# Turning the graph's count matrices by transposing DMAs, with four buffers for the basis loads, in a one-core graph network kernel

## The reference

```
L0: out = relu(concat(segment_sum(h1[src], dst) + img @ Wim + bim,  h1) @ Wap + bap),   h1 = h @ Wn + bn
L1: w[r] = einsum('rb,bio->rio', att, basis)[r]   # basis is 30 x 512 x 512, two relations, two sub-layers
    agg = segment_sum(msg of the edge's own type, row);   out = agg + x @ root + bias
L2: five times relu((h + segment_sum(h[src], dst)) @ W + b)
L3: segment_sum(edge_weight * (x @ weight)[src], dst) + bias
```

## Time and profile before

| | |
|---|---|
| time, median of 3 runs | 2070.17 us (2068.27 to 2072.72) |
| time of the profiled execution | 2070.58 us |
| its span | 2068.6 us |
| TensorE, VectorE, ScalarE busy | 92%, 39%, 30% of the span |
| mean granted TensorE clock | 0.969 |

### The profile page before, as it was taken

The page is one execution under the profiler, slowest core; times in us unless marked ns, Lnnn a source line. Parts: engine busy times, 40 slices in busy tenths (PEclk is TensorE's granted clock), DMA queues, the critical chain, the costliest instruction groups (busy, mean ns, idle before and its releaser), DMA issues.

```text
span 2068.6 us, 23800 instructions
## 1 busy us (share of the span) xinstructions
PE 1900.6 (92%) x7966; PEld 907.6 (44%) x7978; DVE 799.5 (39%) x1978; ACT 626.5 (30%) x1200; POOL 7.8 (0%) x27
## 2 busy tenths in 40 slices
PE   4878888589999989999999999999999999987998
PEld 2545554353333434444444444444444445433443
DVE  5666677424111162110111223354444544384122
ACT  1544544414666042111211000132232323275100
POOL 1000000000000000000000000000000000000000
PEclk9999999879999969999999999999999999998999
DMA  5889889670100052100000010700000000021011
GB/s 119 219 204 228 218 202 224 180 274 0 36 1 1 0 173 102 41 0 1 1 21 31 31 41 31 307 29 5 21 6 21 6 21 1 16 66 56 21 51 41
DMA packets 47379, 157.54 MB, mean 76 GB/s; under 512 B 9316, under 2 KB 11260, under 8 KB 38816
## 3 DMA queue, kind: packets, MB, share of 16 engines
q1 hardware_dynamic: 42880, 142.28, 23.9%
q10 hardware_dynamic: 4384, 13.78, 1.9%
HBM read 120.38 MB, written 35.65 MB: 75 GB/s over the span
## 4 chain that ended last, share of the span: by engine, by line
PE 78%; DMA 7%; DVE 5%; ACT 4%; issue 2%; DVEq 1%; another core or an unknown queue 1%; SPq 0%; POOL 0%; ACTq 0%; POOLq 0%
PE psum L1195 29%; PE psum L1181 28%; PE psum L1413 6%; DMA hs<-in_L_gnn_basis 6%; PE psum L1264 3%; PE psum L1098 2%; PE psum L1317 2%; PE psum L1364 2%; PE psum L1130 2%; PE psum L1129 1%; ACT adj L878 1%; DMA hs<-in_x 1%; DVE hs L582 1%; DVE hs L584 1%
## 5 line engine op out<-in xcount | busy, mean ns | idle before, releaser
L1195 PE MATMUL psum<-hs,adj 128*128 128x512 f16 x2880 | 643.0, 380 | 0.8 <-DVE hs L689 0.8
L1181 PE MATMUL psum<-wb,xt 128*128 128x512 f32 x1152 | 511.6, 602 | 15.5 <-DVE hs L817 13.4
L1195 PEld LDWEIGHTS psum<-hs,adj 128*128 128x128 f16 x2880 | 280.1, 98 | 354.0 <-issue 37.1
L1181 PEld LDWEIGHTS psum<-wb,xt 128*128 128x128 f32 x1152 | 219.2, 193 | 286.0 <-issue 283.9
L970 ACT ACTIVATE adj<-hs,pbias 128x512 f32<-128x512 f32 x216 | 134.5, 708 | 86.1 <-PE psum L1264 86.1
L1130 PE MATMUL psum<-hs 128*128 128x192 f32 x636 | 159.2, 333 | 0.0
L1003 ACT ACTIVATE ua<-ua 128x512 f32<-128x512 f32 x60 | 37.9, 631 | 335.3 <-DVE ua L831 187.6
L582 DVE TENSOR_SCALAR hs<-hs 128x128 f32<-128x128 f16 x318 | 89.8, 282 | 105.7 <-PE psum L1130 63.1
L1413 PE MATMUL psum<-hs,adj 128*128 128x512 f32 x288 | 123.8, 592 | 0.0
L768 DVE TENSOR_TENSOR vt<-psum,adj 128x512 f32<-128x512 f32 x24 | 16.6, 692 | 271.9 <-PE psum L1181 271.9
L1130 PEld LDWEIGHTS psum<-hs 128*128 128x128 f32 x636 | 117.0, 197 | 7.2 <-issue 1.2
(11 more groups left out here) (213 smaller groups left out, 1478.8 us busy)
## 6 DMA issues: line engine op xcount, KB each, us to landing
hs<-in_L_gnn_basis SPq DMA_DIRECT2D x64, 960.0 KB, 8.2
aw_scratch<-xt ACTq DMA_DIRECT2D x12, 768.0 KB, 5.5
adj<-aw_scratch SPq DMA_DIRECT2D x1, 9216.0 KB, 38.1
x_scratch<-adj SPq DMA_DIRECT2D x24, 256.0 KB, 2.2
hs<-x_scratch SPq DMA_DIRECT2D x24, 256.0 KB, 2.6
ts_scratch<-adj SPq DMA_DIRECT2D x1, 4608.0 KB, 17.9
as_scratch<-adj SPq DMA_DIRECT2D x1, 4608.0 KB, 30.1
adj<-ts_scratch SPq DMA_DIRECT2D x1, 4608.0 KB, 14.5
```

The lines of the kernel that those rows point to most:

```text
L1181: x = pe.matmul(psum[:, bank, :], xt[:, i, k, :], w[:, k, :], start=first and k == 0, stop=last and k == 3)
L1195: x = pe.matmul(psum[:, i % 2 + (4 * half if own else 0), :], adj[:, m, j, P * i:P * i + P], hs[:, t, half, j, :], start=n == 1 or (own an ...
```

## The change

**Turning.** A new function `turn_types` issues two transposing DMAs (`dma_start_transpose`, 128 x 1536 float16 each) from ScalarE's queue at the end of each block, from `typed` straight into `adj[:, 1]` and `adj[:, 2]`. TensorE's 24 float16 transposes and ScalarE's four copies of each block go; a block has three turn lots (weights alone) in place of six. ScalarE waits for the transposing DMAs of two blocks before (`typed_turned`) when it stages a block again.

**Buffers.** Two more chunk buffers lie in parts of `adj` that are written late; chunks 0 to 51 go through four buffers, 52 to 63 through the first two. Mixed chunks are staged in four rows in place of two.

**Ahead of the loop.** SP issues three chunk loads at once and the fourth where it issued the first two; the 16 `att` loads move to ScalarE's queue. GpSimd makes the small iotas first; VectorE starts when the edges are there and waits for constants later; `attw` is computed before the window ranges.

**Behind the loop.** The meeting at `built` goes. SP issues the first three loads of `x` when TensorE is through with all turn lots but two; the later loads and stores wait for what they overwrite or read. VectorE waits for the small vectors after the copy of line 601 in place of before it.

```diff
+        for m in (1, 2):
+            basis.append(adj[:, m, NT - 3:NT, :].rearrange("p j n -> p (j n)")[:, 0:4 * D * 2].bitcast(F32))
+        FAR_CHUNKS = 52
+
+        def basis_of(n):
+            return (n + 1) % 4 if n < FAR_CHUNKS else (n + 1) % 2
+
+        def nth_of(n):
+            return len([m for m in range(n + 1) if basis_of(m) == basis_of(n)])
+
+        def follower(n):
+            return min([m for m in range(n + 1, 64) if basis_of(m) == basis_of(n)], default=None)
...
+        spare = wb[:, :, :, :].rearrange("p a b n -> p (a b n)")[:, 2 * NT * P:2 * NT * P + 2 * D].rearrange("p (k n) -> p k n", k=2)
+        mixed = [ua[:, 0, :], ua[:, 1, :], spare[:, 0, :], spare[:, 1, :]]
...
             if s >= 0 and 1 <= q <= 3:
-                here += [("turn", s, 2 * (q - 1)), ("turn", s, 2 * (q - 1) + 1)]
+                here += [("turn", s, q - 1)]
             if u == NW - 1:
-                here += [("turn", BLOCKS - 1, n) for n in range(6)]
+                here += [("turn", BLOCKS - 1, n) for n in range(3)]
...
+            for n in range(3):
+                load_chunk(n)
             sp.wait_ge(ecol_ps, 1)
             sp.wait_ge(span_ready, 4)
-            load_chunk(0)
-            load_chunk(1)
+            load_chunk(3)
             for n in range(CH):
...
-                if n + 2 < CH:
+                if follower(n):
                     sp.wait_ge(side_ps, lot + 1)
-                    load_chunk(n + 2)
+                    load_chunk(follower(n))
                 sp.wait_ge(side_out, side_copied(lot))
...
-            sp.wait_ge(row_out, 16 * (NT + 1))
-            sp.wait_ge(built, 4)
+            sp.wait_ge(side_ps, len(side) - 2)
...
                 if g == 3:
+                    sp.wait_ge(side_ps, len(side))
+                    sp.wait_ge(typed_summed, BLOCKS)
+                    for b in range(2):
+                        sp.wait_ge(typed_turned[b], 16 * BLOCKS)
...
-            dve.wait_ge(c_ready, 7)
             dve.wait_ge(edges_in, 64)
...
+            dve.wait_ge(c_ready, 5)
...
+            dve.wait_ge(c_ready, 6)
+            dve.wait_ge(weights["att"], 16 * 16)
+            step(dve.tensor_reduce(attm[0:120, :], ident[0:120, 0:120].rearrange("p (b j) -> p j b", j=4), AX.X, ALU.add))
...
             x_turned(range(9))
-            dve.wait_ge(weights["small"], 16 * N_SMALL)
             dve.wait_ge(imgt_ps, 1)
             dve.tensor_copy(img_t[:, :, :].rearrange("p k r -> p (k r)"), psum[:, 4, 0:8 * RG]).then_inc(imgt_cp, 1)
+            dve.wait_ge(weights["small"], 16 * N_SMALL)
...
+            def turn_types(s):
+                act.wait_ge(*evicted(PER * s + PER - 1))
+                for t in range(2):
+                    act.dma_start_transpose(adj[:, 1 + t, s, :].rearrange("p (j n) -> p j n", j=NT),
+                                            typed[:, s % 2, t, :, :].rearrange("p j n -> p (j n)")).then_inc(typed_turned[s % 2], 16)
...
                 if u == 0 and s >= 2:
                     act.wait_ge(side_ps, staged_again(s))
+                    act.wait_ge(typed_turned[s % 2], 32 * (s // 2))
...
-                    if q < 3:
-                        for m in range(8):
-                            t, j = divmod(8 * q + m, NT)
-                            x = pe.transpose(bank.bitcast(F16)[:, P * m:P * m + P], typed[:, a % 2, t, j, :], ident16[:])
```

More of the change, by code:

```diff
@@ L220, in program @@
         lsm_neg, lsm_exp = sem("lsm_negmax"), sem("lsm_lnsum")
-        basis_in = [sem(f"basis_in{k}") for k in range(2)]
-        comb_out = [sem(f"comb_out{k}") for k in range(2)]
+        basis_in = [sem(f"basis_in{k}") for k in range(4)]
+        comb_out = [sem(f"comb_out{k}") for k in range(4)]
         act_done = sem("act_done")
@@ L372, in first_of_l1 @@
             def first_of_l1():
-                for k in range(2):
-                    sp.wait_ge(comb_out[k], 64 * 33)
+                for k in range(4):
+                    sp.wait_ge(comb_out[k], 64 * 17)
                 sp.wait_ge(o_ps, tick(0, NT - 1))
@@ L455, in _ @@
                       allow_small_or_imprecise_dtypes=True).then_inc(c_ready, 1)
+            pool.memset(attw[:], 0.0).then_inc(c_ready, 1)
+            pool.iota(iota_s, [[1, REL * TW]], base=0, channel_multiplier=0,
+                      allow_small_or_imprecise_dtypes=True).then_inc(c_ready, 1)
+            pool.memset(zeros, 0.0)
+            pool.tensor_copy(ident16[:], ident[:])
+            pool.memset(ones[:], 1.0)
+            pool.memset(gw[:], 0.0)
+            pool.memset(wa_pad[:], 0.0)
+            pool.memset(bcol[:, 5:6], 1e-5).then_inc(c_ready, 1)
             for k in range(STEP):
                 pool.sem_inc(onehot_free[k], 1)
-            for k in range(2):
+            for k in range(4):
                 pool.sem_inc(comb_out[k], 64)
@@ L538, in _ @@
             dve.tensor_scalar(wcol[0:NW, 3:4], wcol[0:NW, 3:4], 1.0 / STEP, 0.5 - 0.5 / STEP, ALU.mult, ALU.add).then_inc(wcol_ready, 1)
+            dve.wait_ge(c_ready, 6)
+            dve.wait_ge(weights["att"], 16 * 16)
+            step(dve.tensor_reduce(attm[0:120, :], ident[0:120, 0:120].rearrange("p (b j) -> p j b", j=4), AX.X, ALU.add))
+            for l in range(2):
+                for t in range(2):
+                    x = dve.tensor_scalar(attw[0:120, l, 4 * t:4 * t + 4], attm[0:120, :], attc[0:120, l, t:t + 1], None, ALU.mult)
+                x.then_inc(attw_ready, 1)
             dve.wait_ge(wrow_ps, 1)
@@ L551, in _ @@
             dve.wait_ge(ranges_ready, 1)
[L553 to L559, removed]
             def window(w):
@@ L859, in _ @@
         def _(act):
+            for l in range(2):
+                for t in range(2):
+                    for j in range(4):
+                        act.dma_start(attc[j:120:4, l, t:t + 1], ins[f"L1_gnn_att{l + 1}"][t].unsqueeze(1),
+                                      allow_slow_non_contiguous=True).then_inc(weights["att"], 16)
             act.wait_ge(ranges_ready, 1)
@@ L922, in step @@
                 act.wait_ge(act_done, n_act[0])
-            act.wait_ge(built, 4)
-            for k in range(2):
-                act.wait_ge(comb_out[k], 64 * 33)
+            for k in range(4):
+                act.wait_ge(comb_out[k], 64 * 17)
             for i in range(NT):
@@ L1095, in side_lot @@
                     c = a * (CH // 2) + q
-                    pe.wait_ge(basis_in[c % 2], 16 * (c // 2 + 1))
+                    pe.wait_ge(basis_in[basis_of(c)], 16 * nth_of(c))
                     for v in range(4):
-                        x = pe.matmul(bank[32 * v:32 * v + 32, :], attw[0:120, a, :], basis[c % 2][0:120, D * v:D * v + D], start=True, stop=True)
+                        x = pe.matmul(bank[32 * v:32 * v + 32, :], attw[0:120, a, :], basis[basis_of(c)][0:120, D * v:D * v + D], start=True, stop=True)
                 else:
@@ L1103, in side_lot @@
                             pe.wait_ge(*evicted(PER * a + PER - 1 - k))
-                    if q < 3:
-                        for m in range(8):
-                            t, j = divmod(8 * q + m, NT)
-                            x = pe.transpose(bank.bitcast(F16)[:, P * m:P * m + P], typed[:, a % 2, t, j, :], ident16[:])
-                    else:
-                        for m in range(4):
-                            x = pe.transpose(bank[:, P * m:P * m + P], aw_stage[:, a % 2, 4 * (q - 3) + m, :], ident[:])
+                    for m in range(4):
+                        x = pe.transpose(bank[:, P * m:P * m + P], aw_stage[:, a % 2, 4 * q + m, :], ident[:])
                 x.then_inc(side_ps, 1)
```

60 lines of the change are left out of this document (20 added, 40 removed).

## The result

The changed kernel takes 2167.3 us (median of 4 runs, 2140.07 to 2171.88) against 2071.44 us; the ratio is 1.0437, with a 95% interval of 1.0349 to 1.0524. I had said 2046 us, in a range of 2018 to 2086. The sign is wrong.

A forecast was written before the change was run, and what follows sets the result against it. It took two chains of about 300 us, DMA engines and compute engines, to hinder each other in the loop; 14.7 by the loop's end, 6.5 and 3.2 behind it made 24.4 us off, so 2046 us, range 2018 to 2086.

The forecast's parts named there:

- I take 1.5 us: Loop, DMA side: DMA time assumed for each of 24 transposing DMAs, 36 us in all.
- my upper bound of 3.9: Loop, DMA side: most a transposing DMA could take, 3.9 us, from 96 pieces at the `gate_w` loads' 40 ns each.
- the same sum: Loop end: first waiting load at 28.6, plus (291 + 36) us at share 0.97, plus 6 for gaps: 372 us.
- Rival 1: Loop: transposing DMAs are dear, 3.9 us each, decisive from 2.5; 2105 us in all; chance 0.16.
- I price them at nothing: Loop: ScalarE's two DMA issues a block replace its copies, and four staging rows follow the old rule; cost put at zero.
- Rival 2: Loop: transposing DMAs hold ScalarE's queue until landed, 11.2 us a pair, 68 us on the compute side; 2075 us; chance 0.11.
- 17, perhaps 18: Ahead of the loop: time in us when the 16 `att` loads have landed, beside three basis loads.
- 5.5 us sooner: Ahead of the loop: gain at VectorE's first one-hot, contained in the 14.7 us gained by the loop's end.
- my 22.9: Ahead of the loop: forecast time in us of VectorE's first one-hot, in place of 28.39.
- The DMA side without transposing DMAs: Loop: 291 us of DMA time for the remaining loads, engines kept full at share 0.97 by four loads in flight.
- the compute side: Loop: roughly 310 us after late chunks and 20 us of TensorE transposes go, ending at 333, covered by the DMA side.
- Behind the loop, 9.7 us: After the last window: loads of `x` 6.5 us sooner and at most 3.2 us from the `gate_w` wait.

The follow-up runs named there:

- e3: Changed kernel with two plain SBUF-to-SBUF copies of the same bytes in place of each block's two transposing DMAs, type matrices not turned: 2052.98 us, ratio 0.9893.
- e4: Changed kernel with only the first four chunks loaded whole and 64 bytes a row of later ones, DMA engines nearly free: 2026.07 us, one run.
- e2: Kernel before with nothing but the transposing DMAs added, two chunk buffers and old start kept: 2170.89 us, ratio 1.0479.
- e5: Changed kernel with the transposing DMAs issued from SP's queue between chunk loads instead of ScalarE's: 2109.69 us, ratio 1.0173.
- e8: e1 with SP holding back the first three basis loads until the 16 att loads have landed: 2032.15 us, ratio 0.9811.
- e7: e1 with chunk loads behind the first four cut to 64 bytes a row: 2034.31 us, 2 runs.
- e9: e8 with two chunk buffers in place of four, the second load issued where the fourth was: 2055.27 us, ratio 0.9910.
- e1: Changed kernel with float16 blocks turned by TensorE and copied by ScalarE as before, the rest of the change kept: 2040.94 us, ratio 0.9842.
- e6: Changed kernel with four plain copies a block in pieces of 256 bytes in place of two transposing DMAs, type matrices not turned: 2097.90 us, ratio 1.0122.
- e12: Changed kernel with each block's turning cut into eight 128 x 384 transposing DMAs, two behind each of the next four windows: 2213.59 us, ratio 1.0692.
- e10: Changed kernel with each block's turning cut into eight 128 x 384 transposing DMAs, one behind each of the next eight windows: 2228.50 us, ratio 1.0767.

## Why the prediction was wrong

- **"I take 1.5 us", the transposing DMA's DMA time.** This is the first of two steps that failed. 1.5 us is what e3 measures for plain rows, and a transposing one takes 2.3 beside small loads (e4); beside full loads it takes 5.8 here, above even my upper bound of 3.9. I bounded a price per DMA and added it to engines that I had just shown near their limit, as if it stayed the same there. With the measured size and the first waiting load where it came, at 39.9, the same sum gives for the end of the loop 39.9 + (291 + 24 x 5.8) / 0.97 + 6 = 489, and the last window was emptied at 490.4. That hit is luck. The sum has TensorE wait for basis loads, and in the changed kernel it does so for 29.4 us, about as before (27.6), while the chain runs through the holds; and it leaves out the 25 us by which the packets of SP's queue grew. Rival 1, which decides from 2.5 us on, had the direction of the size right and got 0.16; its way, a basis that comes late, is seen in e2 and e5, not in the changed kernel.
- **ScalarE's two issues a block, "I price them at nothing".** This is the second, and in the changed kernel's own chain it is the largest: 108 of 456 us. The staging rows, priced at nothing in the same sentence, have another 36 us there, 7.9%: the stores of mixed chunks landed late. Rival 2 had this hold, at 11.2 us a pair as a fixed price, and 2075. Measured, the hold depends on how full the engines are: 1.7 us in e4, 5.6 in the median and up to 20.9 in the changed kernel. Leaving ScalarE's queue is worth 53 us of the loop (e5), the hold being all or a part of it. I had kept the two rivals apart, and they came together; how the 98 us of the loop divide between them stays open.
- **"17, perhaps 18" for the `att` loads: 5.5 us sooner became 5.6 later.** I moved them past the basis loads in issue order but left them the same engines: they landed in 10 us, not 2 to 3, and the edges were late too (VectorE starts on them at 8.96, in e8 at 6.39). With the order mended (e8) the first one-hot comes at 22.85, my 22.9.
- **The DMA side without transposing DMAs.** I had four buffers keep the engines full, so that 0.97 set the pace. In e8 the share is 0.88 and the compute side sets the end: the loop is 337 us where e7, with hardly any loads, has 332. That the buffers take away the wait for chunks was right, and worth 24 us of the loop (e9). A slip besides: 12 chunks at 0.7 us are 8.4 us, where I put 6.
- **The compute side.** 310 us was said, 312 measured (e4), and 20 us for what leaves TensorE, 20 measured (e7 to e4).
- **Behind the loop, 9.7 us.** It is 10.8 in e1 and 12.8 in e8, but 2.6 in the changed kernel. SP waits for the last transposing DMAs before it loads `wf` and the rest of `x`. I counted 1.5 us for them; in the chain of waits of the changed kernel (start, us, what) their landing has 12.11:

```profile
490.44 1.47 ACTq L902
491.94 12.11 DMA adj<-wb
```

  No run tried this wait by itself. It is not only full engines: in e4, with small loads, the piece behind the loop is 1680.0 us too, 2.9 less than before the change.

On the two rules of the Trainium skill: its 261 GB/s for a transposing DMA (DMA: Bandwidth & Descriptors, Latency and other measured facts) stands against 393,216 bytes in 2.3 us of packet time, 171 GB/s, in e4; the measurement decides. Its advice to turn 128 x 128 blocks on TensorE (VectorE: DVE Perf Modes, Rules for kernel authors) was right for this kernel, though not by its 1309 ns a block: twelve blocks landed in 4.1 us together in e4. The trace agrees with the page on DMA in one more point, that DMAs from different queues run on the same 16 engines (its Rules for kernel authors): `att` loads on ScalarE's queue waited beside basis loads on SP's.

What stays open is why a transposing DMA takes 2.4 us of packet time with half loads and 5.8 with full ones. It isn't the meeting of two queues alone: in e5 it shares SP's queue with the loads, and takes 5.0 us there. Small pieces without turning take 2.5 us of packet time beside full loads (e6), so in packet time it is the turning that suffers; what in it does was not tried. Why the issue of many small pieces holds a queue while the engines are busy is open as well.

## What to carry to other kernels

Before a transfer is added, look at the share of the DMA engines in that very stretch: at 0.69 a transposing DMA was nearly free, where the loads alone took 0.85 it took 4 to 6 us of packet time apiece and held the queue that issued it for 3 to 6 us in the median. So look as well at what else waits in the queue that issues it: on ScalarE's stood the copies that free PSUM, on SP's the basis loads, and each time the chain ran through the holds. A price per DMA taken from a quiet stretch isn't a price in a full one; ask what a busy engine does to the landing of each small load that a chain waits for. And when an edit has several parts, run them apart: here the buffers and the order around the loop win 1.9%, and the headline edit hid it.

## What I had not expected of the hardware

- Issuing a transposing DMA held the queue for 1.3 to 20.9 us, a plain one of the same bytes in rows of 3 KB for 0.5 to 1.1 (e3), and a plain one of half the bytes in pieces of 256 bytes for 0.6 to 9.6 (e6).
- Cutting one into four gave 8.5 us of packet time for 384 KB with two issued a window (e12) and 4.8 with one (e10), against 5.8 uncut: the time hangs on the placing as much as on the cut.
- With transposing DMAs the rate of all DMAs fell as their share rose: 214 GB/s at 0.85 without them (e1), 178 at 0.99 (changed). With plain copies in rows of 3 KB it rose, to 229 at 0.89 (e3).
- TensorE's granted clock in the loop was 0.85 with the long waits, 0.99 before; its count product took 355 ns in the mean in place of 337.
